# Layer 1 attention: the weighted sums of two quads issued in one group instead of one by one

## The chip, the cores and the metric

One Trainium2 chip; the kernel runs on 1 of its cores. The metric is the device time of one execution in microseconds. The kernel before takes 4425.77 us (median of 3 runs, 4424.81 to 4428.68).

## The reference

Two transformer layers over 16 sequences of 512 tokens with 256 features. Layer 0 is an attention block plus a second attention with a mixture of eight experts. The change lies in layer 1, whose attention is

```python
qkv = (x @ w_qkv.T).reshape(B, N, 3, H, D).transpose(2, 0, 3, 1, 4)
q, k, v = (qkv[0], qkv[1], qkv[2])            # 16 heads of 16 features, full (not causal)
q = q * cos + _rotate_half(q) * sin
k = k * cos + _rotate_half(k) * sin
attn = jax.nn.softmax(jnp.einsum('bhqd,bhkd->bhqk', q, k) * scale, axis=-1)
out = jnp.einsum('bhqk,bhkd->bhqd', attn, v)
```

next to a second branch of matrix products with token shift (`r * (relu(k)^2 @ W_v)`). Both branches and the input are added up.

## The kernel before, in words

`two_layers` runs `layer0`, `experts` and `layer1` one after the other. In `layer1` a unit of work is one head and one block of 128 queries against all 512 keys of a batch: 16 heads x 4 query blocks = 64 units per batch (`UNITS`), 16 batches, 1024 units. Four units, the four heads of a group on one query block, are a quad; there are 16 quads per batch (`QUADS`), 256 in all.

Each engine's program is one Python loop over n, the same for all engines. This text calls one pass of it **slot** n, and r is n mod 64, the slot within a batch. Semaphores tie the engines together. In slot n:

- TensorE computes the scores of unit n into one of two PSUM banks (line 1681, `scores`, 512 columns of bf16). It first waits until VectorE has taken the maximum of unit n-2 from that bank.
- VectorE takes the row maximum of unit n (line 1842, `row_max`).
- In every fourth slot TensorE transposes the maxima of a quad (line 1687), which GpSimd has split before, and ScalarE copies them into the query tile (line 1961).
- TensorE computes the scores of unit n-11 again, transposed and with the maximum subtracted (line 1696, `turned_scores`, four matmuls). It waits for the exponentials of unit n-13, which free that bank.
- ScalarE takes the exponentials of unit n-11 into `pts` (line 1968, `exponentials`). `pts` has two places, each for a quad, and the exponentials of quad q wait for the values of quad q-2.
- In slots with r = 0, 4, 8, ... TensorE computes the values of quad (n-16)/4, that is `pts` times the values matrix (line 1710, `values_of`): 16 matmuls in fp32, each with 32 stationary columns, 4 heads side by side in 4 column strips of the array. The trace records each as 2 matmuls, so a quad has 32. They go to one bank `OT`, in which four quads (the four query blocks) stand side by side.

All other work of a batch (projections, rotation, the second branch, the output projection) is spread over chosen slots. On TensorE the projections of 0.9 us each stand in slots such as r = 1, 3, 5, 6, 9, 10, 11, 13, 17, none of them at a multiple of 4; r = 2, 7, 14, 15, 18, 30, 31 and some more have none. On VectorE `turn_out` transposes `OT` and inverts the sums (lines 1863 and 1865) at r = 14, 30, 46 and 62; the rotation products (1852, 1853) stand at r = 4, 7, 11 and 14, the mixes (1857) at 21 to 27, the other sums at 28, 36, 52 and 55. The first quad of a group of four waits until `turn_out` of the group before has read the bank. The line that places the values on TensorE is

```python
q = n - LT - PV
if q % H == 0 and 0 <= q < B * UNITS:
    values_of(q // H)
```

Of the kernel before, what the change touches and what calls it, by code (L numbers as in the profile page):

```python
# [14 lines left out]
F32 = mybir.dt.float32  # L15
# [8 lines left out]
P = 128  # L24
B, T, D = 16, 512, 256
NT = T // P
# [8 lines left out]
QUERY = "hhhmml"  # L35
KEY = "hmlhmh"
STACKS = 9


class Room:  # L40
# [3 lines left out]
def wait(eng, sem, n):  # L44

    if n > 0:
        eng.wait_ge(sem, n)
# [402 lines left out]
def layer0(nc, a, x1_d, xf_d, gt_d, bias_d, K):  # L450

    ctx = ExitStack()
    with ctx:
# [174 lines left out]
        with nc.Block() as block:  # L628
            @block.tensor
            def _(pe):  # L630

                def scores(u):
                    b, g, qt, i = at(u)
                    h, w, to = g * H + i, (qt + 1) * P, S[u % 2]
                    if u % UNITS == 0:
                        pe.wait_ge(s.stacked, 16 * STACKS * (b + 1))
                        wait(pe, s.g_max, UNITS * b)
# [291 lines left out]
            def _(dve):  # L929
# [133 lines left out]
                def scale_rms(c, t):  # L1063
                    if t == 0:
                        dve.wait_ge(s.pow_rms, c + 1)
                        if c > 0:
                            dve.wait_ge(s.stacked, 16 * STACKS * c)
                    nc.vector.tensor_scalar(xr[:, t, :], xn[c % 2][:, t, :], rms[:, t:t + 1], None, ALU.mult).then_inc(s.xr, 1)
# [119 lines left out]
            def _(act):  # L1188
# [89 lines left out]
                def high(c, k):  # L1278
                    act.wait_ge(s.rot_ready, 4 * c + k + 1)
                    if k == 0:  # L1280
                        for half in range(NC):
                            act.wait_ge(s.w_ready, W.count(("xrT", c, half)))
                        wait(act, s.stacked, 16 * STACKS * c)
                    nc.scalar.copy(parts[k][:, 0, :], arena[:, k % 2, :]).then_inc(s.high_done, 1)
# [308 lines left out]
def layer1(nc, a, x1_d, out_d, K, L):  # L1593

    ctx = ExitStack()
    with ctx:
        def sb(name, shape, dt):
            return ctx.enter_context(nc.sbuf_tensor("l1_" + name, shape, dt))
# [11 lines left out]
        H, QUADS = 4, HS * NT // 4  # L1610
        UNITS = HS * NT
# [4 lines left out]
        ident, ident_b, minus_half = K.ident, K.ident_b, K.minus_half  # L1616
        bank = [ps(f"bank{i}", [P, 512], F32) for i in range(8)]
        S, TB, OT, MAXT = bank[0:2], bank[2:4], bank[4], bank[5]
        pts = sb("pts", [P, 2, H, NT, P], F32)
        neg_max = sb("neg_max", [P, 2 * UNITS], F32)  # L1620
        max_rest = sb("max_rest", [P, 2, H], F32)
        recip = sb("recip", [P, T // 32], F32)
# [17 lines left out]
        max_parts, vpad, ks, xnT = L.max_parts, L.vpad, L.ks, L.xnT  # L1640
        cos, sin, w_qkv, w_o, w_rkv, mu, one_mu, b_out = L.cos, L.sin, L.w_qkv, L.w_o, L.w_rkv, L.mu, L.one_mu, L.b_out

        s = Room()
# [18 lines left out]
        def at(u):  # L1662
            return u // UNITS, u % UNITS // (NT * H), u // H % NT, u % H

        def there(c):
            return 0 <= c < B
# [4 lines left out]
        with nc.Block() as block:  # L1671
            @block.tensor
            def _(pe):

                def scores(n):
                    b, g, qt, i = at(n)
                    h = g * H + i
                    if n % UNITS == 0:
                        pe.wait_ge(s.stacked[b % 2], 16 * STACKS * (b // 2 + 1))
                    wait(pe, s.max_ready, n - SB + 1)  # L1680
                    nc.tensor.matmul(S[n % SB][:, :], qs[b % 2][0:96, h, qt * P:(qt + 1) * P], ks[b % 2][0:96, h, :],  # L1681
                                     start=True, stop=True).then_inc(s.scores_ready, 1)

                def turn(q):
                    pe.wait_ge(s.split, 4 * q + 4)
                    wait(pe, s.max_placed, q)
                    nc.tensor.transpose(MAXT[:, 0:P // 2].bitcast(BF16), max_parts[:, q % 2, :], ident_b[:, :]).then_inc(s.max_turned, 1)  # L1687

                def turned_scores(u):
                    b, g, qt, i = at(u)  # L1690
                    h = g * H + i
                    if i == 0:
                        pe.wait_ge(s.max_placed, u // H + 1)
                    wait(pe, s.exp_ready, u - 1)
                    for j in range(NT):
                        m = nc.tensor.matmul(TB[u % 2][:, j * P:(j + 1) * P], ks[b % 2][:, h, j * P:(j + 1) * P], qs[b % 2][:, h, qt * P:(qt + 1) * P],  # L1696
                                             start=True, stop=True)
                    m.then_inc(s.t_ready, 1)

                def values_of(q):  # L1700
                    b, g, qt, _ = at(q * H)
                    pe.wait_ge(s.exp_ready, (q + 1) * H)
                    if qt == 0:
                        wait(pe, s.out_turned, q // NT)
                    if q % QUADS == 0:
                        for half in range(2):
                            pe.wait_ge(*W.emptied(("v", b, half)))
                    for j in range(NT):
                        for i in range(H):
                            m = nc.tensor.matmul(OT[32 * i:32 * (i + 1), qt * P:(qt + 1) * P], vpad[b % 2][:, j, g * H + i, :], pts[:, q % 2, i, j, :],  # L1710
                                                 start=j == 0, stop=j == NT - 1)
                    m.then_inc(s.pv_ready, 1)

# [64 lines left out]
                def fill_out(b, t, k):  # L1778
                    key = ("out", b, t // 2)
                    if t % 2 == 0:  # L1780
                        pe.wait_ge(s.normal, 2 * (b + 1))
                        _, free, n = W.take(key, k)
                        wait(pe, free, n)
                    for half in range(2):
                        ins = nc.tensor.matmul(W.bank(key)[:, (t % 2) * D:(t % 2 + 1) * D], outT[:, out_at(b, half), t * P:(t + 1) * P], w_o[:, half, :],  # L1785
                                               start=half == 0, stop=half == 1)
                    if t % 2:
                        W.full(key, ins)

                for n in range(FIRST, LAST):  # L1790
                    f, r = n // UNITS, n % UNITS
                    c = f + 1
                    if 0 <= n < B * UNITS:
                        scores(n)
                    q = n - (H - 1) - TURN
                    if q % H == 0 and 0 <= q < B * UNITS:
                        turn(q // H)
                    u = n - LT
                    if 0 <= u < B * UNITS:
                        turned_scores(u)  # L1800
                    q = n - LT - PV
                    if q % H == 0 and 0 <= q < B * UNITS:
                        values_of(q // H)
                    if there(f - 1):
                        if r in (23, 26):
                            fill_out(f - 1, (r - 23) // 3, 0)
                        if r in (29, 33):
                            fill_out(f - 1, 2 + (r - 29) // 4, 1)
                    if there(c):
                        if r in (1, 3):  # L1810
                            fill_qk(c, 0, (r - 1) // 2, 1)
                        if r in (5, 6):
                            fill_qk(c, 1, r - 5, 0)
                        if r in (9, 10):
                            fill_qk(c, 2, r - 9, 1)
                        if r in (11, 13):
                            fill_qk(c, 3, (r - 11) // 2, 0)
                        if r in (17, 19):
                            fill_v(c, (r - 17) // 2, 0)
                        if r in (21, 22):  # L1820
                            fill_v(c, r - 19, 1)
                        if r in (37, 38):
                            fill_key(c, 0, r - 37, 0)
                        if r in (39, 41):
                            fill_key(c, 1, (r - 39) // 2, 1)
                        if r in (42, 43):
                            fill_rec(c, r - 42, 0)
                        if r in (45, 47):
                            fill_rec(c, 2 + (r - 45) // 2, 1)
                        if r in (49, 51):  # L1830
                            fill_val(c, (r - 49) // 2, 0)
                        if r in (53, 54):
                            fill_val(c, r - 51, 1)
                    if there(c + 1) and r in (57, 58):
                        fill_xT(c + 1, r - 57, r - 57)
# [120 lines left out]
            def _(act):  # L1956
# [7 lines left out]
                def exponentials(u):  # L1964
                    q = u // H
                    act.wait_ge(s.t_ready, u + 1)
                    wait(act, s.pv_ready, q - 1)
                    nc.scalar.activation(pts[:, q % 2, u % H, :, :], TB[u % 2][:, :].rearrange("p (j q) -> p j q", j=NT),  # L1968
                                         ACT.Exp, scale=DS ** -0.5).then_inc(s.exp_ready, 1)

                def high(c, k):
                    act.wait_ge(s.rot_ready, 4 * c + k + 1)
                    if k == 0 and c > 0:
                        act.wait_ge(s.stacked[(c - 1) % 2], 16 * STACKS * ((c - 1) // 2 + 1))
                    nc.scalar.copy(parts[k][:, 0, :], turned[k // 2][k % 2][:, :]).then_inc(s.high_done, 1)
# [38 lines left out]
                for n in range(FIRST, LAST):  # L2014
                    f, r = n // UNITS, n % UNITS
                    c = f + 1
                    q = n - (H - 1) - TURN
                    if q % H == 0 and 0 <= q < B * UNITS:
                        place(q // H)
                    u = n - LT  # L2020
# [331 lines left out]
```

## Time and profile before

| | |
|---|---|
| median of 3 runs | 4425.77 us |
| profiled execution, its own time | 4434.39 us |
| its span, first to last instruction | 4432.3 us |
| mean granted TensorE clock | 0.961 |
| busy: TensorE, VectorE, ScalarE, GpSimd | 89%, 66%, 58%, 58% of the span |
| layer 1 | 3215 to 4432 us of the span |

The profile is of one execution. Layer 1 is periodic: from the second batch on each batch takes 77.0 us. Times in the timeline are microseconds from the start of the span. A matmul's recorded duration overlaps with the next ones, so what a matmul costs the engine is read from the distance between starts.

### The profile page before, as it was taken

The page shows a single profiled execution, that of the slowest core. Times are in us where ns is not written, and L with a number is a line of the kernel's source. Part 1 is how long each engine was busy: PE and PEld are TensorE (multiplying, and loading weights), DVE is VectorE, ACT ScalarE, POOL GpSimd, SP SyncE. Part 2 cuts the span into 40 slices and gives each one's busy share as a digit, 9 for nine tenths or more (in the row PEclk, how much of TensorE's full clock was granted, in tenths as well). Part 3 has the DMA queues.
Part 4 walks back from the last instruction along what each step waited for, and adds up shares of the span by engine and source line. Part 5 has one row for each costly group of instructions (what it writes and reads, how often), then busy time and mean ns, then how long its engine had stood idle before and what let it go on. Part 6 is the DMA issues. An engine that isn't in the chain of part 4 may idle for free. (4 is left out here: it accounts for less than half of the span.)

```text
span 4432.3 us, 105538 instructions
## 1 busy us (share of the span) xinstructions
PE 3956.8 (89%) x37596; PEld 2587.9 (58%) x37596; DVE 2912.0 (66%) x8565; ACT 2581.4 (58%) x6209; POOL 2586.2 (58%) x4110
## 2 busy tenths in 40 slices
PE   3999999999999999999999999928599999999999
PEld 1555555555555655555555555526366666666666
DVE  5666575665665666656656656553287777878786
ACT  2656556556566565565565655602277777777776
POOL 4658567577486575675765755724454545555452
PEclk8999999999999999999999999969799999999999
DMA  5324323333243233342432332122332332424231
GB/s 126 79 70 90 71 74 88 73 87 81 64 97 74 75 78 77 82 91 62 98 77 68 88 73 66 58 100 56 55 61 52 55 58 50 67 47 66 49 53 27
DMA packets 168566, 317.07 MB, mean 72 GB/s; under 512 B 21680, under 2 KB 112112, under 8 KB 162928
## 3 DMA queue, kind: packets, MB, share of 16 engines
q1 hardware_dynamic: 162928, 300.88, 31.7%
q0 software_dynamic: 3968, 5.25, 0.7%
q8 instruction: 306, 5.01, 0.5%
q10 hardware_dynamic: 1152, 4.19, 0.3%
q14 instruction: 212, 1.74, 0.2%
HBM read 126.66 MB, written 32.59 MB: 36 GB/s over the span
## 5 line engine op out<-in xcount | busy, mean ns | idle before, releaser
L1395 POOL TENSOR_SCALAR l_prob_wo<-l_prob_wo,l_recip_g 128x128 f32<-128x128 f32 (+3 forms) x1024 | 1095.6, 1088 | 237.3 <-DVE l_recip_g L971 236.8
L1842 DVE TENSOR_REDUCE l_neg_max<-l_bank 128x1 f32<-128x512 f32 x1024 | 680.4, 684 | 260.5 <-PE l_bank L1681 259.0
L1968 ACT ACTIVATE l_pts<-l_bank 128x512 f32<-128x512 f32 x1024 | 593.3, 597 | 297.5 <-PE l_bank L1696 288.7
L952 DVE CUSTOM_DVE_ANT_0 l_bank<-l_bank,l_mask 128x128 f32<-128x128 f32 (+3 forms) x1024 | 502.6, 498 | 388.6 <-PE l_bank L639 381.2
L965 DVE CUSTOM_DVE_ANT_0 l_prob_wo<-l_bank,l_bias 128x128 f32<-128x128 f32 (+3 forms) x1024 | 476.7, 484 | 415.5 <-PE l_bank L690 391.7
L1223 ACT ACTIVATE l_prob_wo<-l_prob_wo,l_neg_max_g 128x128 f32<-128x128 f32 (+3 forms) x1024 | 571.0, 559 | 293.5 <-DVE l_neg_max_g L965 290.2
L1215 ACT ACTIVATE l_pts<-l_bank 128x128 f32<-128x128 f32 (+3 forms) x1024 | 438.3, 437 | 460.9 <-PE l_bank L657 445.3
L701 PE MATMUL l_bank<-ident,l_prob_wo 128*128 128x128 f32 x2560 | 432.4, 283 | 94.3 <-POOL l_prob_wo L1395 42.9
L701 PEld LDWEIGHTS l_bank<-ident,l_prob_wo 128*128 128x128 f32 x2560 | 287.7, 141 | 334.4 <-POOL l_prob_wo L1395 191.1
L1681 PE MATMUL l_bank<-next_ks,l_qs 96*128 96x512 bf16 x1024 | 393.5, 385 | 45.5 <-DVE l_neg_max L1842 23.2
L1696 PEld LDWEIGHTS l_bank<-l_qs,next_ks 128*128 128x128 bf16 x4096 | 303.5, 97 | 181.2 <-ACT l_pts L1968 30.6
L1383 POOL CAST l_max_parts<-l_neg_max 128x4 bf16<-128x4 f32 x256 | 49.4, 193 | 615.8 <-DVE l_neg_max L952 615.5
L1696 PE MATMUL l_bank<-l_qs,next_ks 128*128 128x128 bf16 x4096 | 395.4, 218 | 0.9 <-ACT l_pts L1968 0.7
L639 PE MATMUL l_bank<-l_ks,l_qs 96*128 96x128 bf16 (+3 forms) x1024 | 308.7, 306 | 74.4 <-DVE l_neg_max L952 63.2
L2056 POOL CAST next_max_parts<-l_neg_max 128x4 bf16<-128x4 f32 x256 | 71.2, 278 | 515.0 <-DVE l_neg_max L1842 515.0
L690 PE MATMUL l_bank<-l_kT,l_qT 64*128 64x128 f32 (+3 forms) x2048 | 352.8, 460 | 0.0
L718 PE MATMUL l_bank<-l_pts,l_v 128*64 128x256 f32 (+1 forms) x3072 | 347.5, 363 | 2.6 <-ACT l_pts L1233 0.8
L732 PE MATMUL l_bank<-l_xnT,l_w 128*128 128x512 f32 x640 | 339.9, 614 | 0.0
L656 PE MATMUL l_bank<-l_qs,l_ks 128*128 128x128 bf16 x2560 | 319.1, 226 | 21.9 <-ACT l_pts L1215 21.8
L980 DVE COPY l_pts<-l_bank 128x128 f32<-128x128 f32 (+3 forms) x512 | 246.8, 482 | 99.2 <-PE l_bank L701 80.9
L656 PEld LDWEIGHTS l_bank<-l_qs,l_ks 128*128 128x128 bf16 x2560 | 204.7, 102 | 168.9 <-ACT l_pts L1215 70.7
L755 PE MATMUL l_bank<-l_prob_wo,l_outT 128*128 128x256 f32 x1024 | 284.3, 404 | 12.5 <-DVE l_bias L1003 9.2
(264 smaller groups left out, 8019.4 us busy)
## 6 DMA issues: line engine op xcount, KB each, us to landing
l_bias<-bias SPq DMA_DIRECT2D x128, 512.0 KB, 4.5
l_qs<-l_parts SPq DMA_DIRECT2D x192, 128.0 KB
l_qs<-l_qs SPq DMA_DIRECT2D x96, 256.0 KB
l_x<-in_x SPq DMA_DIRECT2D x32, 512.0 KB, 4.6
l_kT<-l_bias SPq DMA_DIRECT2D x128, 128.0 KB, 3.3
l_qT<-l_arena SPq DMA_DIRECT2D x128, 128.0 KB, 3.3
l_qT<-l_bias SPq DMA_DIRECT2D x128, 128.0 KB, 3.0
l_prob_wo<-in_Wo SPq DMA_DIRECT2D x16, 1024.0 KB, 4.8
```

What stands on the lines that cost most here:

```text
L656: m = nc.tensor.matmul(to[:, j * P:(j + 1) * P], ks[:, h, j * P:(j + 1) * P], qs[:, h, qt * P:(qt + 1) * P], start=True, stop=j < qt)
L690: nc.tensor.matmul(G4[(v + i) % 4][:, 0:w], qT[half, g, qt * P:(qt + 1) * P], kT[half, g // 2, 0:w], start=True, stop=True).then_inc(s.g_s ...
L701: m = nc.tensor.transpose(PT[i][:, j * P:(j + 1) * P], prob[qt][:, i, j * P:(j + 1) * P], ident[:, :])
L952: nc.vector.tensor_tensor_reduce(S[u % 2][:, 0:w], S[u % 2][:, 0:w], mask[:, T - w:T], -1.0, 3.0e38, ALU.add, ALU.min, neg_max[:, k:k + 1] ...
L965: nc.vector.tensor_tensor_reduce(prob[qt][:, i, :], G4[v % 4][:, 0:w], bias[:, g % 2, i, T - w:T], -1.0 / ROOT, 3.0e38, ALU.add, ALU.min, ...
L1215: nc.scalar.activation(pts[:, q % 2, i, 0:w, :], TB[u % 2][:, 0:w * P].rearrange("p (j q) -> p j q", j=w), ACT.Exp, scale=DS ** -0.5).then ...
L1223: nc.scalar.activation(prob[qt][:, i, :], prob[qt][:, i, :], ACT.Exp, bias=neg_max_g[:, k:k + 1], scale=-1.0, accum_out=sums_g[:, k:k + 1] ...
L1395: nc.gpsimd.tensor_scalar(prob[qt][:, i, :], prob[qt][:, i, :], recip_g[:, k:k + 1], None, ALU.mult).then_inc(s.g_scaled, 1)
L1681: nc.tensor.matmul(S[n % SB][:, :], qs[b % 2][0:96, h, qt * P:(qt + 1) * P], ks[b % 2][0:96, h, :], start=True, stop=True).then_inc(s.scor ...
L1696: m = nc.tensor.matmul(TB[u % 2][:, j * P:(j + 1) * P], ks[b % 2][:, h, j * P:(j + 1) * P], qs[b % 2][:, h, qt * P:(qt + 1) * P], start=Tr ...
L1842: nc.vector.tensor_reduce(neg_max[:, n % (2 * UNITS):n % (2 * UNITS) + 1], S[n % SB][:, :], AX.X, ALU.max, negate=True).then_inc(s.max_rea ...
L1968: nc.scalar.activation(pts[:, q % 2, u % H, :, :], TB[u % 2][:, :].rearrange("p (j q) -> p j q", j=NT), ACT.Exp, scale=DS ** -0.5).then_in ...
```

## The change

The values of two neighbouring quads, 2k and 2k+1, are issued together, in the slot in which quad 2k+1 had its turn. The even quad so moves four slots back; slots with r = 0, 8, 16, ..., 56 now have no values and r = 4, 12, ..., 60 have those of two quads. `pts` gets three places in place of two, and the exponentials of quad q wait for the values of quad q-3.

```diff
+QUAD_RING = 3
...
-        pts = sb("pts", [P, 2, H, NT, P], F32)
+        pts = sb("pts", [P, QUAD_RING, H, NT, P], F32)
...
-                            m = nc.tensor.matmul(OT[32 * i:32 * (i + 1), qt * P:(qt + 1) * P], vpad[b % 2][:, j, g * H + i, :], pts[:, q % 2, i, j, :],
+                            m = nc.tensor.matmul(OT[32 * i:32 * (i + 1), qt * P:(qt + 1) * P], vpad[b % 2][:, j, g * H + i, :], pts[:, q % QUAD_RING, i, j, :],
...
                     q = n - LT - PV
-                    if q % H == 0 and 0 <= q < B * UNITS:
+                    if q % (2 * H) == H and 0 <= q < B * UNITS:
+                        values_of(q // H - 1)
                         values_of(q // H)
...
-                    wait(act, s.pv_ready, q - 1)
-                    nc.scalar.activation(pts[:, q % 2, u % H, :, :], TB[u % 2][:, :].rearrange("p (j q) -> p j q", j=NT),
+                    wait(act, s.pv_ready, q + 1 - QUAD_RING)
+                    nc.scalar.activation(pts[:, q % QUAD_RING, u % H, :, :], TB[u % 2][:, :].rearrange("p (j q) -> p j q", j=NT),
```

Line numbers after the first hunk grow by one, behind the second insertion by two. The order of instructions changes on TensorE alone. Here it is around r = 14 to 17, before (line 1681 begins a slot, 1687 is the transpose of maxima in r = 15, 1696 the turned scores, 1710 the values, 1739 a projection of the values matrix):

```order
L1681 MATMUL l_bank<-next_ks,l_qs 128x512
L1696 MATMUL l_bank<-l_qs,next_ks 128x128 x4
L1681 MATMUL l_bank<-next_ks,l_qs 128x512
L1687 MATMUL l_bank<-ident_b,next_max_parts 128x128
L1696 MATMUL l_bank<-l_qs,next_ks 128x128 x4
L1681 MATMUL l_bank<-next_ks,l_qs 128x512
L1696 MATMUL l_bank<-l_qs,next_ks 128x128 x4
L1710 MATMUL l_bank<-l_pts,next_vpad 32x128 x16
L1681 MATMUL l_bank<-next_ks,l_qs 128x512
L1696 MATMUL l_bank<-l_qs,next_ks 128x128 x4
L1739 MATMUL l_bank<-next_w_qkv,next_xnT 128x256 x2
```

and now:

```order
L1682 MATMUL l_bank<-next_ks,l_qs 128x512
L1697 MATMUL l_bank<-l_qs,next_ks 128x128 x4
L1682 MATMUL l_bank<-next_ks,l_qs 128x512
L1688 MATMUL l_bank<-ident_b,next_max_parts 128x128
L1697 MATMUL l_bank<-l_qs,next_ks 128x128 x4
L1682 MATMUL l_bank<-next_ks,l_qs 128x512
L1697 MATMUL l_bank<-l_qs,next_ks 128x128 x4
L1682 MATMUL l_bank<-next_ks,l_qs 128x512
L1697 MATMUL l_bank<-l_qs,next_ks 128x128 x4
L1740 MATMUL l_bank<-next_w_qkv,next_xnT 128x256 x2
```

The values are gone from r = 16: between the turned scores of r = 13 and the projection in r = 17 nothing but scores and turned scores is left. Four slots on, at r = 20, before:

```order
L1681 MATMUL l_bank<-next_ks,l_qs 128x512
L1696 MATMUL l_bank<-l_qs,next_ks 128x128 x4
L1710 MATMUL l_bank<-l_pts,next_vpad 32x128 x16
L1681 MATMUL l_bank<-next_ks,l_qs 128x512
L1696 MATMUL l_bank<-l_qs,next_ks 128x128 x4
L1739 MATMUL l_bank<-next_w_qkv,next_xnT 128x256 x2
```

and now:

```order
L1682 MATMUL l_bank<-next_ks,l_qs 128x512
L1697 MATMUL l_bank<-l_qs,next_ks 128x128 x4
L1711 MATMUL l_bank<-l_pts,next_vpad 32x128 x32
L1682 MATMUL l_bank<-next_ks,l_qs 128x512
L1697 MATMUL l_bank<-l_qs,next_ks 128x128 x4
L1740 MATMUL l_bank<-next_w_qkv,next_xnT 128x256 x2
```

The group is twice as long, 32 matmuls in place of 16.

## Rows read from the trace of the kernel before

**Rows 1.** the page, part 1: busy time, share of the span, instructions.

```profile
PE 3956.8 (89%) x37596; PEld 2587.9 (58%) x37596; DVE 2912.0 (66%) x8565; ACT 2581.4 (58%) x6209; POOL 2586.2 (58%) x4110
```

**Rows 2.** windows, one batch: stretch, length, busy by engine, PEclk, DMA, GB/s.

```profile
3814.88:3891.90 77.02, 75.10 (x944) 51.56 (x945) 61.54 (x105) 55.89 (x100) 39.53 (x89) 1.00 0.36 56
```

**Rows 3.** timeline, PE, r = 8: start, length, engine, line, operation.

```profile
3824.51 0.38 PE L1681 MATMUL l_bank<-next_ks,l_qs 96*128 96x512 bf16 x1
...
3825.05 1.08 PE L1710 MATMUL l_bank<-l_pts,next_vpad 128*32 128x128 f32 x32
3826.06 0.39 PE L1681 MATMUL l_bank<-next_ks,l_qs 96*128 96x512 bf16 x1
```

**Rows 4.** timeline, PE, two narrow stretches inside one group of values.

```profile
3803.74 0.73 PE L1710 MATMUL l_bank<-l_pts,next_vpad 128*32 128x128 f32 x20
...
3804.18 0.29 PE L1710 MATMUL l_bank<-l_pts,next_vpad 128*32 128x128 f32 x4
```

**Rows 5.** timeline, PE, r = 0 to 3: the score matmuls that begin the slots.

```profile
3814.88 0.38 PE L1681 MATMUL l_bank<-next_ks,l_qs 96*128 96x512 bf16 x1
...
3816.51 0.39 PE L1681 MATMUL l_bank<-next_ks,l_qs 96*128 96x512 bf16 x1
...
3817.88 0.38 PE L1681 MATMUL l_bank<-next_ks,l_qs 96*128 96x512 bf16 x1
...
3818.32 0.38 PE L1681 MATMUL l_bank<-next_ks,l_qs 96*128 96x512 bf16 x1
```

**Rows 6.** timeline, DVE, r = 0: maxima of r = 63 and 0.

```profile
3815.56 1.22 DVE L1842 TENSOR_REDUCE l_neg_max<-l_bank 128x1 f32<-128x512 f32 x2
```

**Rows 7.** timeline, DVE: maximum of r = 7, then of 8 and 9.

```profile
3824.43 0.69 DVE L1842 TENSOR_REDUCE l_neg_max<-l_bank 128x1 f32<-128x512 f32 x1 [0.67 <-PE l_bank L1681]
...
3826.23 1.28 DVE L1842 TENSOR_REDUCE l_neg_max<-l_bank 128x1 f32<-128x512 f32 x2
```

**Rows 8.** timeline, PE, r = 16 and 17.

```profile
3834.28 0.39 PE L1681 MATMUL l_bank<-next_ks,l_qs 96*128 96x512 bf16 x1
3834.50 0.39 PE L1696 MATMUL l_bank<-l_qs,next_ks 128*128 128x128 bf16 x4
...
3836.93 0.39 PE L1681 MATMUL l_bank<-next_ks,l_qs 96*128 96x512 bf16 x1 [0.90 <-DVE l_neg_max L1842]
```

**Rows 9.** timeline, DVE, r = 16: maxima of r = 15 and 16.

```profile
3836.18 1.28 DVE L1842 TENSOR_REDUCE l_neg_max<-l_bank 128x1 f32<-128x512 f32 x2
```

**Rows 10.** timeline: PE, r = 32 and 33; DVE, maxima of 31 and 32.

```profile
3854.60 0.39 PE L1681 MATMUL l_bank<-next_ks,l_qs 96*128 96x512 bf16 x1
...
3856.38 0.39 PE L1681 MATMUL l_bank<-next_ks,l_qs 96*128 96x512 bf16 x1
...
3855.65 1.26 DVE L1842 TENSOR_REDUCE l_neg_max<-l_bank 128x1 f32<-128x512 f32 x2
```

**Rows 11.** timeline: PE r = 48, DVE maximum 47; PE r = 58, DVE maximum 56.

```profile
3875.09 0.38 PE L1681 MATMUL l_bank<-next_ks,l_qs 96*128 96x512 bf16 x1
...
3875.16 1.22 DVE L1842 TENSOR_REDUCE l_neg_max<-l_bank 128x1 f32<-128x512 f32 x2
...
3887.10 0.38 PE L1681 MATMUL l_bank<-next_ks,l_qs 96*128 96x512 bf16 x1
...
3885.78 0.68 DVE L1842 TENSOR_REDUCE l_neg_max<-l_bank 128x1 f32<-128x512 f32 x1
```

**Rows 12.** timeline, PE: the values of the last quad.

```profile
4419.35 1.08 PE L1710 MATMUL l_bank<-l_pts,next_vpad 128*32 128x128 f32 x32 [0.95 <-ACT l_pts L1968]
```

**Rows 13.** timeline and windows, layer 0: two waits of PE, the clock behind.

```profile
1499.33 0.23 PE L639 MATMUL l_bank<-l_ks,l_qs 96*128 96x128 bf16 x1 [2.04 <-DVE l_neg_max L952]
...
1500.44:1503.85 3.41, 3.41 (x17) 2.74 (x16) 1.12 (x8) 1.28 (x3) 3.05 (x3) 0.54 0.16 35
...
1150.82 0.23 PE L639 MATMUL l_bank<-l_ks,l_qs 96*128 96x128 bf16 x1 [1.45 <-DVE l_neg_max L952]
...
1151.00:1161.00 10.00, 10.00 (x110) 8.05 (x107) 6.16 (x25) 5.08 (x10) 6.37 (x15) 1.00 0.41 108
```

## The prediction, made before the changed kernel ran

> **What bounds the kernel now.** I read the page first: TensorE is busy 89% of the span, VectorE 66% [rows 1]. The change touches layer 1 alone, so the share that counts is that of one of its batches: in 77.02 us TensorE is busy 75.1 us, VectorE 61.5, ScalarE 55.9, at full clock [rows 2]. TensorE is the bound on average, and a group of values costs its time. But VectorE has 61.5/64 = 0.96 us of work per slot, and a slot of TensorE is uneven: 1.63, 1.37 and 0.44 us for r = 0, 1 and 2 [rows 5], that is with values, with a projection, and with scores and turned scores alone. In short slots TensorE is the faster of the two and, with two score banks, may run ahead by two units at most; so the third thing to read is who waits in each stretch. In the timeline at r = 16 TensorE starts its scores at 3834.28, and those of r = 17 at 3836.93, 2.65 us later, with 0.90 us put down to the maximum on VectorE [rows 8]. The long slots pay for VectorE's backlog. The change takes values out of every second one of them.
>
> **What merging saves.** The values slot r = 8 takes 3826.06 - 3824.51 = 1.55 us [rows 3], a bare slot 0.44 [rows 5]: a quad costs 1.11. Its first matmul starts 0.54 after the slot begins, 0.10 later than the next slot would in a bare one. Inside, matmuls start in eight rounds of four, a round each (3804.18 - 3803.74)/4 = 0.11 us [rows 4], so 0.88 for eight; from the first start to the next scores it is 1.01 [rows 3], 0.13 more. Entering and leaving a group cost 0.10 + 0.13 = 0.23 us. If the rounds run through from one quad to the next, each of the 128 pairs saves this once: 128 x 0.23 = **29 us less** of TensorE work. The second quad's wait for its exponentials covers units whose exponentials the turned scores of the same slot have waited for already, so it adds nothing; its first matmuls go to other columns of the same bank. At r = 0, 16, 32 and 48 the first quad of four no longer waits for `turn_out`; that wait stands before a longer one in all places but r = 0, and is in the terms below.
>
> **What the move costs.** The even quad's 1.11 us leaves r = 0, 8, ..., 56 and comes back four slots later, where all is bound by TensorE (scores two slots ahead, VectorE idle before each maximum). What counts is how much earlier the next slots start. A score matmul starts at the earliest 0.07 us after the end of the maximum two units before (3836.18 + 0.68 = 3836.86 against 3836.93 [rows 8, 9]).
> - r = 16: the scores of r = 17 wait for the maximum of r = 15. It ends at 3836.86 because VectorE has `turn_out` and two products before it, none of which hangs on the moved values. They start at 3836.93 as before. Lost 1.11.
> - r = 32: the maximum of r = 31 starts at 3855.65, ends some 0.66 on, the scores of r = 33 start at 3856.38 [rows 10], and can start no earlier. Lost 1.11.
> - r = 0: the maximum of r = 63 starts at 3815.56 and ends 0.62 later [rows 6]; the scores of r = 1 can start at 3816.25 in place of 3816.51 [rows 5]. Gained 0.26, lost 0.85.
> - r = 8: the maximum of r = 8 stands behind the products and ends at 3826.23 + 0.67 = 3826.90 [rows 7]. The scores of r = 10 can start at 3826.97; now they do at 3826.06 + 1.37 = 3827.43 [rows 3, 5]. Gained 0.46, lost 0.65.
> - r = 56: the maximum of r = 56 ends at 3885.78 + 0.69 = 3886.47, so the scores of r = 58 can start at 3886.54 in place of 3887.10 [rows 11]. Lost 0.55.
> - r = 48: the maximum of r = 47 ends at 3875.16 + 0.62 = 3875.78; the scores of r = 49 can start at 3875.85, not 3875.09 + 0.44 = 3875.53 [rows 11]. Lost 0.32.
> - r = 24 and r = 40: no row shows these without values; the bounds are 0 and 1.11. At r = 40 projections fill the slots around and VectorE is idle before each maximum, so 0. At r = 24 the mixes make VectorE late two slots on; I take 0.14.
>
> Sum: (1.11 + 1.11 + 0.55 + 0.32 + 0.14) x 16 = 51.7 and (0.85 + 0.65) x 15, since the last batch has no scores behind it, = 22.5, together **74 us lost**. At the end the last quad waits 0.95 us for its exponentials [rows 12]; the quad before it was done under such waits and now stands in the open: 1.11 - 0.23 = 0.9 at most, 0.7 taken. Net 74.2 - 29.4 + 0.7 = **45 us more**, 2.8 us a batch.
>
> The third place in `pts` is needed for the move and costs nothing by itself: exponentials of quad q now wait for quad q-3, whose pair is issued at least three slots before. SP and GpSimd keep their order; the split of maxima and the rotation hang on VectorE and shift with it. DMAs are issued as before.
>
> **The clock.** At r = 16 TensorE's last turned-scores matmul ends at 3834.50 + 0.39 = 3834.89, and without values nothing follows until 3836.93: it is idle for 2.04 us [rows 8]. Layer 0 has a wait of just this length, 2.04 us before 1499.33, and the stretch 1500.44 to 1503.85 then runs at a granted clock of 0.54, the lower level of 1.2 GHz but for its edge; behind a wait of 1.45 us the next 10 us stay at 1.00, that is 2.4 GHz [rows 13]. A fall of 3.41 us costs up to half of it, 1.7 us, as the slots behind r = 16 are bound by TensorE. The 2.04 us of layer 0 stand between shorter, sparser groups of matmuls than those here, so I take a fall in 8 of the 15 or 16 batches, 8 x 1.7 = **14 us**; the bounds are 0 and 16 x 1.7 = 27 us. The Trainium skill's page "TensorE: Matmul & The Clock Gate" (section "Why this matters for your kernels") advises against idle gaps clearly longer than this one only; by it the clock would stay, and the sum would be the 45 us. The row of layer 0 speaks against that.
>
> Sum: 45 + 14 = 59 us. The profiled execution took 4434.4, so it would be 4493; the median of the runs stands 8.6 lower, 4425.8 + 59 = **4485 us**, slower by 1.3%.
>
> **Rivals.**
> 1. The same waits, but the clock stays at its upper level: 4425.8 + 45 = 4471. For it: layer 1 is denser than layer 0 around its waits, and its clock is 1.00 throughout [rows 2]. Against: the 2.04 us row.
> 2. Faster: the short slots are no obstacle, because the maxima come early enough once the four slots before them have been lengthened by a double group (VectorE clears its backlog in r = 12 and 28 before it comes to r = 16 and 32). It decides at the maxima of r = 15 and 31: were they to end more than 1.1 us earlier, the merge would keep its 29 us: 4396. Against it: VectorE is late there not by backlog but by the operations between the maxima of r = 14 and r = 15, and the former starts when TensorE delivers. It could also hold in part. The Trainium skill's page "TensorEngine Tiling (Array Packing)" (section "Key Properties") says that a change of tiling mode drains the array. By that rule alone the change takes out 128 drains and gives the same 4396; the 0.23 us above are that drain, and what the rule leaves out is VectorE.
> 3. Gain and loss cancel, about 4426: lost slots at r = 16 and 32 alone count, 2.2 x 16 = 36 against 29. It needs r = 0, 8, 48 and 56 to lose nothing, against the four rows above.
> 4. The merge does not do what it says: the wait between the two quads splits the group and the 0.23 us stays. Then 29 us come on top: 4500 with the clock steady, 4514 with it falling.
>
> **How the numbers follow.** Forecast (waits and falling clock) 0.50; rival 1 0.31; rival 4 0.06; rival 2 0.08; rival 3 0.05. The forecast's own range is 45 - 8 to 45 + 27 + 4 us, 4463 to 4502; rival 1 spans 4463 to 4479. Rival 4 is taken in up to its lower end, and rivals 2 and 3 are left out: 4458 to 4503. A difference of 0.2%, 9 us, is about what a measurement of this kernel can tell from none. Faster 0.08, same 0.05, slower 0.87.
>
> **What would show it.** In the profile after: groups of 64 matmuls 1.9 us long from first start to the next scores; a batch of 79.8 us with full clock and up to 81.5 with a fall; the scores of r = 17 about 2.65 us behind those of r = 16 with an idle time near 2.0 us before them; TensorE's waits for the maxima longer by some 4.6 us a batch (74 us over 16); VectorE's busy time unchanged and its share lower; a granted clock below 1.00 in some slices of layer 1. The forecast is wrong if a batch takes under 77 us, if the distance from r = 16 to r = 17 shrinks by the 1.1 us of the values, or if the clock column of layer 1 stays at 9 while the time still rises by more than 53 us.

## The result and the profile after

The changed kernel takes 4486.88 us (median of 4 runs, 4482.19 to 4492.42) against 4427.23 us for the kernel before (4 runs): ratio 1.0128, 95% interval 1.0115 to 1.0142. It is slower by 1.3%. Run again on another chip it came out at 4495.59 us, ratio 1.0134 (1.0117 to 1.0151). The profiled execution took 4492.42 us, span 4490.3.

The first line of the page of the profile, as [rows 1]: the work is the same, spread over more time.

```profile
PE 3959.7 (88%) x37596; PEld 2604.0 (58%) x37596; DVE 2903.3 (65%) x8565; ACT 2578.1 (57%) x6209; POOL 2587.8 (58%) x4110
```

Two neighbouring batches of layer 1 in the view of windows, as [rows 2] (stretch, length, busy time by engine, PEclk, DMA, GB/s), and the stretch behind r = 16 of the second:

```profile
3923.86:4003.61 79.75, 74.35 (x944) 51.92 (x945) 60.81 (x105) 55.73 (x100) 39.98 (x89) 1.00 0.34 54
3842.46:3923.86 81.40, 76.01 (x944) 52.97 (x945) 60.95 (x105) 55.73 (x100) 39.47 (x89) 0.98 0.34 54
...
3866.75:3870.16 3.41, 3.41 (x16) 2.42 (x15) 2.00 (x3) 2.31 (x5) 3.41 (x4) 0.50 0.33 74
```

A batch took 77.02 us. It now takes 79.75 us at full clock, or 81.40 us where the clock stands at its lower level, 0.50, for 3.41 us. Both were forecast. TensorE is even busy for less time than the 75.10 us of [rows 2] when the clock stays: 74.35.

The timeline of TensorE at r = 44, then at r = 15 to 17 of the same batch, as [rows 3, 8]:

```profile
3980.72 0.38 PE L1682 MATMUL l_bank<-next_ks,l_qs 96*128 96x512 bf16 x1
3980.94 0.39 PE L1697 MATMUL l_bank<-l_qs,next_ks 128*128 128x128 bf16 x4
3981.26 1.95 PE L1711 MATMUL l_bank<-l_pts,next_vpad 128*32 128x128 f32 x64
3983.14 0.39 PE L1682 MATMUL l_bank<-next_ks,l_qs 96*128 96x512 bf16 x1
...
3943.57 0.38 PE L1682 MATMUL l_bank<-next_ks,l_qs 96*128 96x512 bf16 x1
...
3944.29 0.39 PE L1682 MATMUL l_bank<-next_ks,l_qs 96*128 96x512 bf16 x1
3944.51 0.39 PE L1697 MATMUL l_bank<-l_qs,next_ks 128*128 128x128 bf16 x4
3946.94 0.39 PE L1682 MATMUL l_bank<-next_ks,l_qs 96*128 96x512 bf16 x1 [2.04 <-DVE l_neg_max L1844]
```

The merge works: the slot with two quads is 3983.14 - 3980.72 = 2.42 us long, and two slots of 1.55 less a bare one of 0.44 would be 2.66. So 0.24 us is saved per pair, and the 64 matmuls go through without a seam (1.88 us from the first start to the next scores). At r = 16 the values are gone and the slot is as long as before: 2.65 us from one scores to the next, of which TensorE now idles 2.04.

VectorE in that stretch, as [rows 9]:

```profile
3944.15 0.70 DVE L1865 STREAM_TRANSPOSE l_blocks<-l_bank 128x512 f32<-128x512 f32 x1
3944.89 0.25 DVE L1867 RECIPROCAL l_recip<-l_blocks 128x16 f32<-128x16 f32 x1
3945.06 0.63 DVE L1854 TENSOR_TENSOR l_turned<-l_bank,next_cos 128x512 f32<-128x512 f32 x1
3945.60 0.68 DVE L1855 TENSOR_TENSOR l_turned<-l_bank,next_sin 128x512 f32<-128x512 f32 x1
3946.20 1.87 DVE L1844 TENSOR_REDUCE l_neg_max<-l_bank 128x1 f32<-128x512 f32 x3
```

It works without a gap, starting with `turn_out` 0.14 us before the scores of r = 16. The maximum of r = 15, the first of the three, starts 1.91 us behind those scores; before it was 3836.18 - 3834.28 = 1.90 [rows 8, 9]. So the wait has taken the place of the values, and their 1.11 us are the loss of this pair.

### The profile page after: what moved, and what is told of

The parts are those of the page before. It is cut to its first block and busy times, and to the rows that moved or that the text cites. A ratio compares the mean times of both kernels' runs of the same rounds, so it can differ in the third digit from the quotient of the medians.

```text
span 4490.3 us, 105534 instructions
## 1 busy us (share of the span) xinstructions
PE 3959.7 (88%) x37596; PEld 2604.0 (58%) x37596; DVE 2903.3 (65%) x8565; ACT 2578.1 (57%) x6209; POOL 2587.8 (58%) x4110
## 5 line engine op out<-in xcount | busy, mean ns | idle before, releaser
L1682 PE MATMUL l_bank<-next_ks,l_qs 96*128 96x512 bf16 x1024 | 398.2, 389 | 97.3 <-DVE l_neg_max L1844 71.5
```

## The experiments

The run of the kernel before beside which each was timed differs by some 10 us from one chip to the next (medians 4427 to 4437), so small differences are read from the ratio, and from the length of a batch in the profile (79.75 us for the changed kernel, 77.03 before).

### The third place alone

```diff
-                    if q % (2 * H) == H and 0 <= q < B * UNITS:
-                        values_of(q // H - 1)
+                    if q % H == 0 and 0 <= q < B * UNITS:
                         values_of(q // H)
```

> The kernel before with three places in the ring of exponentials and nothing moved. My theory gives the third place no part in the loss: 4427 us as before, within 9 us, and 77.0 us a batch. The rival, that the larger ring (other addresses, a looser wait of ScalarE) costs or gives something of its own, would show as more than 9 us either way.

Measured: 4436.71 us beside 4436.76, ratio 1.0005 (0.9995 to 1.0014), a batch of 77.03 us. The ring has no part in it.

### The same move without the merge

```diff
+                    q = n - LT - PV
+                    if q % (2 * H) == H and 0 <= q < B * UNITS:
+                        values_of(q // H - 1)
                     u = n - LT
                     if 0 <= u < B * UNITS:
                         turned_scores(u)
-                    q = n - LT - PV
                     if q % (2 * H) == H and 0 <= q < B * UNITS:
-                        values_of(q // H - 1)
                         values_of(q // H)
```

> The changed kernel, but in the slots r = 4, 12, ..., 60 the even quad's values stand before the turned scores and the odd quad's behind them: the same move, no merge. If entering and leaving a group costs 0.23 us, this is 128 x 0.23 = 29 us slower than the changed kernel: 4516 us, and a batch without a fall of the clock takes 79.74 + 1.87 = 81.6 us. If what matters is the move alone and the array drains for nothing, it stays at 4487.

Measured: 4514.49 us, ratio 1.0182 (1.0163 to 1.0200). The window of one batch at full clock, and TensorE at r = 44:

```profile
3934.28:4015.95 81.67, 76.28 (x944) 50.89 (x945) 60.84 (x105) 56.07 (x100) 40.02 (x89) 1.00 0.33 53
```

```profile
3992.34 0.38 PE L1682 MATMUL l_bank<-next_ks,l_qs 96*128 96x512 bf16 x1
3992.65 1.08 PE L1711 MATMUL l_bank<-l_pts,next_vpad 128*32 128x128 f32 x32
3993.67 0.40 PE L1697 MATMUL l_bank<-l_qs,next_ks 128*128 128x128 bf16 x4
3993.99 1.08 PE L1711 MATMUL l_bank<-l_pts,next_vpad 128*32 128x128 f32 x32
3995.01 0.39 PE L1682 MATMUL l_bank<-next_ks,l_qs 96*128 96x512 bf16 x1
```

A batch is 81.67 - 79.75 = 1.92 us longer than with the merge, 0.24 us for each of its 8 pairs; the slot is 2.67 us in place of 2.42. The price of entering and leaving a group is shown from both sides; what in the array makes it, no run shows. The whole time is only some 21 to 24 us above what the two ratios of the changed kernel stand for, not the 29 expected. In this profile TensorE idles 2.03 us before the scores of r = 17 just as in the changed kernel, but only 4 of those 14 waits have a fall of the clock behind them, not 9, and a fall costs 1.4 to 1.7 us.

### The maximum made short, without and with the change

The maximum is taken over 128 of the 512 keys, so these two kernels do not compute the reference. In both kernels:

```diff
-... S[n % SB][:, :], AX.X, ALU.max,
+... S[n % SB][:, 0:128], AX.X, ALU.max,
...
-                                         ACT.Exp, scale=DS ** -0.5).then_inc(s.exp_ready, 1)
+                                         ACT.Exp, scale=1e-5).then_inc(s.exp_ready, 1)
```

> The kernel before with the row maximum taken over 128 of the 512 keys (and the exponential's factor made tiny, so that all stays finite): VectorE's 0.68 us per unit becomes about 0.3, the rest is as it was. TensorE's waits of some 3 us a batch go: about 77.0 - 3 = 74 us a batch, 4380 us. It is the base for the next run.

> The changed kernel with the same short row maximum. My theory: with VectorE out of the way the move costs nothing and the merge keeps its 0.23 us per pair, so it is 29 us faster than short_max_before (about 4351 us), and no clock falls in the batches. Rival: the move costs by itself (ScalarE starved by the long groups, the clock, the ring), then it is slower than short_max_before as well, by up to 60 us.

Measured: without the change 4404.23 us, ratio to before 0.9929 (0.9913 to 0.9946); with it 4428.82 us, 0.9983 (0.9972 to 0.9994). The first expectation was met in part: a batch is 74.79 us, 2.2 us shorter in place of 3, and the time 4404 and not 4380. The second failed: the changed form was to be 29 us faster than this base and is 25 us slower. One batch of it, as a window, and what TensorE waited for in it (engine, line, waited for: us in total, times, longest):

```profile
3890.45:3967.28 76.83, 73.70 (x947) 51.31 (x945) 37.14 (x105) 55.77 (x100) 39.96 (x89) 1.00 0.36 56
```

```profile
PEld l_bank L1697 <- ACT l_pts L1970: 5.6, 14, 0.8
PEld l_bank L1682 <- DVE l_neg_max L1844: 5.0, 14, 1.5
```

VectorE's busy time fell from 60.8 to 37.1 us, and still the batch is 2.04 us longer than its base, so the move itself costs 2.04 + 8 x 0.24 = 4.0 us a batch, against 4.7 with long maxima. Two things had been left out of my working. At r = 16 it is not the maximum itself that is long, but `turn_out` and the products in front of it, and they had not been shortened: TensorE still idles 1.32 us before the scores of r = 17 and 0.46 before those of r = 33. And behind the maxima stands the next engine: turned scores wait for the exponentials of the unit two slots before. At r = 9, where the changed kernel waits 0.21 us for ScalarE, the short kernel waits 0.45, in its timeline:

```profile
3900.95 0.38 PE L1682 MATMUL l_bank<-next_ks,l_qs 96*128 96x512 bf16 x1
3901.78 0.40 PE L1697 MATMUL l_bank<-l_qs,next_ks 128*128 128x128 bf16 x4 [0.45 <-ACT l_pts L1970]
```

### Maximum and exponentials short

Beside the two edits above (here in the changed kernel; the kernel before gets the same, and `pts` is set to a constant once, ahead of the loop):

```diff
-                    nc.scalar.activation(pts[:, q % QUAD_RING, u % H, :, :], TB[u % 2][:, :].rearrange("p (j q) -> p j q", j=NT),
+                    nc.scalar.activation(pts[:, q % QUAD_RING, u % H, 0:1, :], TB[u % 2][:, 0:P].rearrange("p (j q) -> p j q", j=1),
```

> short_max_before with the exponentials, too, over 128 of the 512 columns (the rest of the ring is a constant set at the start of the layer): ScalarE's 0.60 us per unit becomes about 0.3. TensorE waited 1.1 us a batch there, little of it for ScalarE: 74.5 to 74.8 us a batch. It is the base for the next run.

> The changed kernel with both short. In short_max_after, a batch of 76.8 us, 1.7 us were waits of the turned scores for exponentials (r = 1, 9, 57) and 2.1 us waits for maxima behind turn_out and products at r = 16 and 32. If ScalarE is what took VectorE's place, the 1.7 us go and 2.1 stay: about 75.1 us a batch, within 0.6 us of short_both_before. If ScalarE is not it, the batch stays at 76.8.

Measured: 4382.72 us without the change, ratio 0.9883 (0.9862 to 0.9903), and 4394.57 with it, 0.9911 (0.9894 to 0.9929). One batch of each in the windows, first without the change, then with it:

```profile
3865.26:3939.54 74.28, 73.83 (x948) 51.18 (x945) 37.86 (x105) 35.87 (x100) 39.65 (x89) 1.00 0.37 58
```

```profile
3872.21:3947.33 75.12, 72.61 (x948) 51.77 (x945) 37.56 (x105) 35.87 (x99) 39.90 (x89) 1.00 0.37 58
```

75.12 us, as expected, and 0.84 us over its base, not 0.6; the base itself came out a little under its 74.5 to 74.8. Taking ScalarE's load away brings 1.7 us a batch with the change and 0.5 without it, so ScalarE did stand behind VectorE. The 0.84 is what is left after the merge's 1.92: by the starts of the scores the move still costs 1.11 us at r = 16, 0.76 at r = 32, 0.44 at r = 0 and 0.25 each at r = 8 and 56, and nothing any more at r = 24, 40 and 48. At r = 16, 32 and 0 `turn_out` stands in VectorE's way, at r = 16 the products too. In the timeline TensorE idles 1.46 us before the scores of r = 17, for a maximum that is itself 0.3 us long.

```profile
3893.60 0.39 PE L1682 MATMUL l_bank<-next_ks,l_qs 96*128 96x512 bf16 x1 [1.46 <-DVE l_neg_max L1844]
```

### The wait at r = 16 filled with matmuls of no use

```diff
+                    if r == 16 and 0 <= u < B * UNITS:
+                        for _ in range(12):
+                            nc.tensor.matmul(MAXT[0:96, 128:512], ident_b[:, 0:96], ks[(n // UNITS) % 2][:, 0, 0:384], start=True, stop=True)
                     q = n - LT - PV
```

> The changed kernel with 12 matmuls of 384 columns without use (into columns of the maxima's bank that nobody reads) in each slot r = 16, about 1.9 us inside the 2.2 us that TensorE waits there. If the falling clock is what makes 81.4 us of a 79.74 us batch, no batch has a fall, every one takes 79.7 to 79.9 us, and the kernel is about 15 us faster than the changed one (4472 us), though TensorE does more. If the clock has nothing to do with the wait, the 81.4 us batches stay, or all get longer by up to 1.9 us.

Measured: 4477.89 us, ratio 1.0104 (1.0086 to 1.0123), so 11 to 13 us less than the changed kernel's two ratios stand for. In its profile 12 of the 13 batches from the second to the fourteenth take 79.74 to 79.76 us; none has a fall, and the one of 81.66 us is long for another reason (below). A batch, and r = 16 in it:

```profile
3912.15:3991.90 79.75, 76.30 (x957) 53.29 (x958) 60.86 (x105) 55.77 (x100) 40.00 (x89) 1.00 0.35 54
```

```profile
3932.82 0.39 PE L1697 MATMUL l_bank<-l_qs,next_ks 128*128 128x128 bf16 x4
3933.04 2.11 PE L1804 MATMUL l_bank<-next_ks,ident_b 128*96 128x384 bf16 x12
3935.24 0.39 PE L1682 MATMUL l_bank<-next_ks,l_qs 96*128 96x512 bf16 x1
```

More work for TensorE, the same distance of 2.65 us from r = 16 to r = 17, and a faster kernel: the falls behind r = 16 come from the idle time. Each cost 81.40 - 79.75 = 1.65 us. In the first batch two falls remain, which the changed kernel has too. They do not stand behind r = 16 but behind shorter waits, of 1.26 us before the scores of r = 28 and 1.17 before those of r = 33; the first of them in the changed kernel:

```profile
3231.62 0.40 PE L1682 MATMUL l_bank<-next_ks,l_qs 96*128 96x512 bf16 x1 [1.26 <-DVE l_neg_max L1844]
```

The kernel before waits 1.05 us there, and has no fall.

### One pair taken apart

Only r = 16 and r = 20 keep their quads in slots of their own:

```diff
-                    if q % (2 * H) == H and 0 <= q < B * UNITS:
-                        values_of(q // H - 1)
-                        values_of(q // H)
+                    if q % H == 0 and 0 <= q < B * UNITS:
+                        if r in (4, 12, 28, 36, 44, 52, 60):
+                            values_of(q // H - 1)
+                            values_of(q // H)
+                        elif r + 4 not in (4, 12, 28, 36, 44, 52, 60):
+                            values_of(q // H)
```

> The changed kernel, but the two quads of r = 16 and r = 20 stay in slots of their own as before; the other seven pairs stay merged. My price for this pair is 1.11 lost against 0.23 saved: a batch of 79.74 - 0.88 = 78.87 us. The wait at r = 16 falls back to 1.1 us, so no clock falls either: 14 + 15 = 29 us faster than the changed kernel, 4458 us. Rival: the loss is spread evenly over the pairs, then it is 1/8 of 60 = 7 us faster only.

Measured: 4461.89 us, ratio 1.0065 (1.0046 to 1.0083). A batch takes 78.88 us, 0.87 less, and none behind the first has a fall. The 29 us expected from it are 28 by the ratio against the first measurement (31 against the second). Half of the loss of 1.28% goes with one pair of eight.

### Only the two pairs for which the move is free

The same form with `(28, 44)`.

> The kernel before with a third place in the ring and only the pairs of r = 28 and r = 44 merged, where by my sum the move costs 0.14 and 0. The merge then keeps 0.10 + 0.23 us: a batch of 76.65 to 76.70 us against 77.03, in all 5 to 6 us faster than before (ratio 0.9987). Rival, after what the short maximum showed (the move costs even when the maxima are fast): no gain, 77.0 us or more a batch.

Measured: 4426.66 us beside 4433.66, ratio 0.9981 (0.9972 to 0.9991), a batch of 76.55 us. So 0.48 us a batch is won, more than the 0.33 to 0.38 expected: it is 2 x 0.24, and the move costs nothing at r = 24 either. Where TensorE has work in the slots around, the merge keeps what it saves; the rival of this expectation falls.

### VectorE's work moved in place of TensorE's

```diff
-                        if r == 14:
+                        if r == 13:
                             turn_out(f - 1, 3)
...
-                        if r in (30, 46, 62):
-                            turn_out(f, (r - 30) // 16)
+                        if r in (29, 45, 62):
+                            turn_out(f, (29, 45, 62).index(r))
...
-                        if r in (25, 27):
-                            mix(c, 0, (r - 25) // 2)
+                        if r in (24, 27):
+                            mix(c, 0, (r - 24) // 3)
```

with the values alone in their slots but for the pair of r = 44.

> Meant to be faster than both: the values stand alone, except for the pair of r = 44, and VectorE's work is moved off the short slots instead: turn_out from r = 14, 30, 46 to 13, 29, 45, and the mix of r = 25 to 24. By the same arithmetic the scores of r = 17 start about 0.7 us earlier, the wait of 0.7 at r = 27 goes, r = 31 and 32 gain up to 0.4, the pair gives 0.23: a batch of 75.0 to 75.6 us, 25 to 32 us faster than before (ratio 0.993 to 0.994). If VectorE's backlog only moves to the next short slots, a batch stays at 76.8 or above.

Measured: 4422.88 us, ratio 0.9970 (0.9959 to 0.9981), a batch of 75.91 us, not 75.0 to 75.6. `turn_out` at r = 29 makes the maximum of r = 30 late, and the wait behind r = 31 (of the weight load ahead of the next scores) grows from 0.23 to 0.84 us. So it went back to 30:

> vector_moved with turn_out back at r = 30 in place of 29, where it had made the wait at r = 31 grow from 0.23 to 0.84 us. The waits at r = 31 and 32 fall back to 0.45 us in all: a batch of 75.5 us in place of 75.9, 6 us faster than vector_moved, some 24 us under before (ratio 0.9945).

Measured: 4420.66 us beside 4437.08, ratio 0.9967 (0.9954 to 0.9980); a batch takes 75.52 us, as expected. TensorE at r = 16 and 17:

```profile
3903.42 0.39 PE L1682 MATMUL l_bank<-next_ks,l_qs 96*128 96x512 bf16 x1 [0.16 <-DVE l_neg_max L1847]
...
3903.96 1.08 PE L1711 MATMUL l_bank<-l_pts,next_vpad 128*32 128x128 f32 x32
3905.21 0.39 PE L1682 MATMUL l_bank<-next_ks,l_qs 96*128 96x512 bf16 x1 [0.16 <-DVE l_neg_max L1847]
```

1.79 us from one scores to the next, where it was 2.65 in both kernels. Of the 1.51 us that a batch gains, 0.24 come from the merged pair of r = 44, 0.76 from r = 15 and 16 and 0.69 from r = 27, where the moved `mix` stood in the way; 0.18 are lost at r = 29. The time, though, fell by 15 us and not by 24: fourteen batches of 1.51 us are 21, but in this profile the third took 82.98 us, 7.5 too many (below), and the last is 1.6 us longer than before. This kernel is faster than both others.

## Why the prediction was right

**What merging saves**: 0.23 us a pair in the prediction, 0.24 measured in the changed kernel and again in the one with two groups. The rounds run through, so rival 4 falls.

**What the move costs**: term by term, from score starts of the batch at 3923.86 and of the batch of [rows 2] in the kernel before.

| | lost, predicted | lost, measured |
|---|---|---|
| r = 16 | 1.11 | 1.11 (slot 2.65 before and after) |
| r = 32 | 1.11 | 1.11 (1.78 before and after) |
| r = 0 | 0.85 | 0.84 (slot 1.37, was 1.63) |
| r = 8 | 0.65 | 0.65 (r = 8 to 10: 2.46, was 2.92) |
| r = 56 | 0.55 | 0.57 (r = 56 to 58: 1.91, was 2.44) |
| r = 48 | 0.32 | 0.32 (slot 0.76, was 1.55) |
| r = 24 | 0.14 | 0.08 (r = 24 to 28: 3.53, was 4.56) |
| r = 40 | 0 | 0 |

The sum is 4.68 us a batch against 4.73 predicted; less 8 x 0.24 it is 2.76, and the batches differ by 2.73. The weak terms were r = 24, which no row bounded well and whose 0.08 is given back in the slot before it (1.42, was 1.50), and the first batch, for which I had made no term: it grew from 71.5 to 77.2 us, 3.2 of it by two falls of the clock. One sign did not come out as told: TensorE's waits for the maxima were to be 4.6 us a batch longer, but its whole idle time grew by (79.75 - 74.35) - (77.02 - 75.10) = 3.5 only.

**The clock**: 8 falls of 1.7 us predicted. Of the 16 batches, 14 have the wait of 2.04 us (in the first it is 1.18, in the last 0.84); 9 of these 14 have a fall behind it, of 1.65 us, and two more stand in the first batch, of 1.6. In both profiles of the changed kernel 11 stand at these places. The row of layer 0 was the right guide and rival 1, with the advice of the Trainium skill's page "TensorE: Matmul & The Clock Gate" (section "Why this matters for your kernels") beside it, the wrong one: these waits are shorter than those that the advice forbids, and the clock fell. That the falls would come only in part of the batches was a choice without a row, so that 8 lies this close to 9 is luck.

**The sum**: the first and the last scores of layer 1 lie 4409.6 - 3202.7 = 1206.9 us apart before (the first ones stand a little ahead of the 3215 us where the table begins layer 1) and 4467.6 - 3200.5 = 1267.1 after: 60.2 us, where 59 were predicted and the medians show 59.7. The sum is closer than its terms: without the falls the batches lost 43.7 us (45 predicted), the 11 falls cost 18 (14 predicted), and 1.5 are missing since one batch of the profile before was itself long (last section). That these cancel to about 1 us is luck too; the path and the two causes are not.

**What the prediction had wrong** is in its account of rival 2, not in its number. It let the merge keep its whole gain once the maxima came early enough, and named them as the only gate. With the maxima short the changed kernel is still 2 us a batch slower than its base, since `turn_out` and products stand before them and since exponentials gate the turned scores. For a kernel with fast maxima I expected 29 us less from the merge, and it lost 25.

What stays open is why 9 of 14 equal waits have a fall behind them, and which. A second profile of the changed kernel was expected to have its falls in other batches; it has 9 again, 8 of them in the same batches. With two groups the same wait, in batches 1.92 us longer, has 4. Nor is 2 us a bound: the first batch has falls behind 1.26 and 1.17 us, while none of the 14 waits of 1.46 us with maximum and exponentials short has one. No run varied the place of the wait alone.

## What to carry to other kernels

When an engine is the bound on average, ask slot by slot which of its work fills time that it would otherwise spend waiting. Work taken out of such a slot does not make the next one start earlier; it costs up to its full length where it comes back, as 1.11 us did at r = 16 and 32 to save 0.24. Merge groups only where the engine has other work around the slot that is emptied, and where it waits, move the other engine's work instead. And an idle time of about 2 us on TensorE has a second price: it can pull the clock down for the work behind, as it did here after 9 of 14 waits of 2.04 us.

## What else the runs showed

In the third batch of the last kernel TensorE stands still for 4.29 us with no releaser in the profile ("issue"), and the clock falls behind it. The row of the timeline, and in the windows the 4.29 us and what follows:

```profile
3397.09 2.05 PE L1751 MATMUL l_bank<-l_mixT,next_w_rkv 128*128 128x512 f32 x2 [4.29 <-issue]
```

```profile
3392.80:3397.09 4.29, 0.00 (x1) 0.03 (x1) 0.96 (x6) 0.60 (x1) 1.02 (x1) 0.91 0.69 99
3397.09:3403.90 6.81, 6.81 (x18) 3.12 (x19) 1.38 (x2) 2.10 (x4) 0.65 (x4) 0.55 0.90 172
```

This is why that batch took 82.98 us. Leaving out what falls behind r = 16 make, batches longer than their neighbours by 1.5 to 7.5 us stand in 7 of the 14 profiles, each time the third, fourth or seventh batch, and the extra time lies between r = 37 and 42. The kernel before has one too (78.5 in place of 77.0 us), the changed kernel none. No run tells what stops TensorE there.
